# A Mamba layer on one core: eight units' products with B made by ScalarE and TensorE from u turned, instead of five by matmuls with diagonals

## What is computed

```
xi = silu(conv(in_proj(x)));  dt, Bm, Cm = split(x_proj(xi));  dt = softplus(dt_proj(dt) + dt_b)
dA  = exp(dt[..., None] * A)                      # (b, t, 512, 16)
dBx = (dt * xi)[..., None] * Bm[:, :, None, :]    # u = dt * xi
h_t = dA_t * h_(t-1) + dBx_t;   y_t = sum over the 16 states of h_t * C_t
y   = (y + xi * D) * silu(z);   out_proj, sigmoid
```

## Time and profile before

| | us |
|---|---|
| median of 3 runs (lowest, highest) | 4762.65 (4761.55, 4768.12) |
| span of the profiled execution, first to last instruction | 4760.7 |
| both passes of the Mamba layer, from 82 on | 3338 |
| a chunk of the backward pass, one of the forward pass | 105.5, 103.2 |
| join and feed-forward net | 1341 |

### The profile page before, as it was taken

One profiled execution on the slowest core, in us unless ns is written; L12 is line 12 of the kernel. 1 busy time (PEld: TensorE's weight loads), 2 busy tenths in 40 slices (PEclk: granted clock), 3 DMA queues, 4 the chain that ended last, 5 costly groups with the idle time before them and its releaser, 6 DMA issues. The chain is left out here.

```text
span 4760.7 us, 67108 instructions
## 1 busy us (share of the span) xinstructions
PE 4479.5 (94%) x24932; PEld 3395.1 (71%) x24932; DVE 3894.2 (82%) x4126; ACT 3109.7 (65%) x5158; POOL 3320.9 (70%) x1559
## 2 busy tenths in 40 slices
PE   7999999999999989999999999998799999999999
PEld 3666666666666666667666667666688888888888
DVE  5999999999999999999999999999854444444452
ACT  6777777777777777777777777777444444444443
POOL 4999999999999999999999999999820000000000
PEclk9999999999999999999999999999999999999999
DMA  7544444444444444444444444444231111010100
GB/s 271 178 142 141 134 151 132 136 134 134 143 139 134 155 132 138 129 139 139 131 147 140 129 130 136 143 142 156 103 123 32 36 32 36 32 36 32 36 23 10
DMA packets 297736, 545.76 MB, mean 115 GB/s; under 512 B 101888, under 2 KB 186624, under 8 KB 262784
## 3 DMA queue, kind: packets, MB, share of 16 engines
q1 hardware_dynamic: 296512, 529.91, 35.6%
q10 hardware_dynamic: 896, 11.54, 0.7%
HBM read 502.77 MB, written 50.14 MB: 116 GB/s over the span
## 5 line engine op out<-in xcount | busy, mean ns | idle before, releaser
L1400 DVE TENSOR_TENSOR_SCAN m_h<-bank,m_state,m_dBx 128x512 f32<-128x512 f32 x1512 | 1841.2, 1265 | 35.0 <-ACT bank L1145 27.2
L868 PEld LDWEIGHTS bank<-ident,m_h 128*128 128x128 f32 x8192 | 980.9, 143 | 417.2 <-issue 345.8
L868 PE MATMUL bank<-ident,m_h 128*128 128x128 f32 x8192 | 1197.6, 276 | 12.9 <-DVE m_h L1408 12.8
L1283 POOL TENSOR_TENSOR m_dBx<-u,m_Bs 128x1024 f32<-128x1024 f32 x432 | 1016.4, 2377 | 0.4 <-DMA m_Bs<-b_dram 0.2
L1283 POOL TENSOR_TENSOR m_dBx<-m_u,m_Bs 128x1024 f32<-128x1024 f32 x432 | 1015.5, 2371 | 1.2 <-DMA m_Bs<-b_dram 1.0
L1294 POOL TENSOR_TENSOR m_h<-m_h,m_Cs 128x1024 f32<-128x1024 f32 x384 | 909.4, 2368 | 105.8 <-ACT m_state L1077 105.1
L1408 DVE TENSOR_TENSOR m_h<-m_h,bank 128x1024 f32<-128x1024 f32 x640 | 767.0, 1198 | 51.7 <-PE bank L850 51.4
L1145 ACT ACTIVATE bank<-m_dt,cols 128x512 f32<-128x512 f32 x864 | 584.8, 688 | 225.2 <-DVE m_h L1400 223.7
L1145 ACT ACTIVATE bank<-dt,cols 128x512 f32<-128x512 f32 x864 | 584.1, 688 | 193.6 <-DVE m_h L1400 191.6
L302 POOL TENSOR_TENSOR mvj<-mvj,norm_c 128x4 f32<-128x4 f32 x16 | 16.5, 1032 | 969.0 <-DVE mvj L263 969.0
L731 PE MATMUL bank<-hT,w_in 128*128 128x512 f32 x1024 | 547.4, 630 | 113.1 <-ACT hT L998 105.8
(11 more groups left out here) (177 smaller groups left out, 5847.1 us busy)
## 6 DMA issues: line engine op xcount, KB each, us to landing
m_Bs<-b_dram SPq DMA_DIRECT2D x256, 1024.0 KB, 6.3
m_Cs<-c_dram SPq DMA_DIRECT2D x384, 256.0 KB, 3.7
m_dg<-d_dram SPq DMA_DIRECT2D x160, 256.0 KB, 3.9
xx<-in_x SPq DMA_DIRECT2D x16, 512.0 KB, 4.9
xn_dram<-xx SPq DMA_DIRECT2D x16, 512.0 KB, 4.5
yb_dram<-m_ysb SPq DMA_DIRECT2D x16, 512.0 KB, 5.0
xx<-xn_dram SPq DMA_DIRECT2D x16, 512.0 KB, 3.8
x_dram<-m_ysb SPq DMA_DIRECT2D x16, 512.0 KB, 5.0
```

Of the source, the lines that this page charges most:

```text
L868: mm = pe.matmul(YB[b][:, o:o + P], h[:, k % NH, m, tok:tok + P], ident[:, :], start=(s == 0 and o == 0), stop=False, is_transpose=True, s ...
L1283: pool.tensor_tensor(dBx[:, dbx_ring(ch, k) % NDBX, :, :], u[ch.batch][:, m, :], Bs[:, k // BP % 2, k % BP, :].unsqueeze(1).broadcast_to(( ...
L1400: dve.tensor_tensor_scan(o, decays, share, initial, ALU.mult, ALU.add).then_inc(S["scan"], 1)
```

## The change

- `A_UNITS` is now eight units, four in each half: 8, 11, 14 and 18, 21, 24, 27, 30. GpSimd makes 24 B products for a chunk (27 before).
- `P_UNITS` goes from 12 to 14 units. VectorE makes 18 C products (20 before), GpSimd 14.
- No diagonals: `store_diagonals`, `load_d`, the tensor `d_dram` and its first filling go. In their place ScalarE scales uT by B, which now lies along the partitions as a column of `Ct`: four ACTIVATEs of 128 x 256 for a unit (`scale_u`), at slots 2k - 5 to 2k - 2, into `uB`. TensorE turns uB back into the PSUM bank at slots 2k - 2 and 2k - 1 (`fill_a`).
- u of both halves is turned: two more turns by TensorE, two more copies by ScalarE.
- SyncE's list is in another order, without the loads and stores of diagonals.

```diff
-      J_Y: (45, 60, 14, 17), J_OUT: (31, 40), J_UT: (25, 26)}
+      J_Y: (45, 60, 14, 17), J_OUT: (31, 40), J_UT: (25, 26), J_UZ: (5, 7)}
+TURNS = ((J_UZ, AT_UZ), (J_UT, AT_UT))
-P_UNITS = (2, 3, 5, 9, 13, 15, 16, 19, 20, 22, 23, 27)
-A_FIRST, A_STEP, NA = 19, 3, 5
-A_UNITS = tuple(A_FIRST + A_STEP * i for i in range(NA))
+P_UNITS = (1, 4, 5, 7, 9, 11, 13, 16, 17, 20, 21, 23, 27, 29)
+A_UNITS = (8, 11, 14, 18, 21, 24, 27, 30)
+NA = len(A_UNITS)
+AT_US = (-5, -4, -3, -2)
...
                 load_c(ch, 4)
+                if norms(ch, 2):
+                    store_xn(ch.go(2))
                 load_b(ch, 4)
                 load_c(ch, 5)
-                load_b(ch, 5)
                 load_c(ch, 6)
-                if norms(ch, 2):
-                    store_xn(ch.go(2))
-                load_c(ch, 7)
-                load_b(ch, 6)
                 if has(ch, 1):
                     store_b(ch.go(1))
-                load_d(ch, 2)
+                load_b(ch, 5)
+                load_c(ch, 7)
                 load_c(ch, 8)
+                load_b(ch, 6)
...
                     if m == 0:
-                        if i == 0:
-                            wait_drained(pe, ch, J_UT[1])
-                        pe.wait_ge(d_in[n % NDG], 16 * (n // NDG) + 16)
+                        pe.wait_ge(S["u_scaled"], n + 1)
                     pe.wait_ge(S["scan"], tile - NDA + 1)
                     for s in range(TS):
-                        mm = pe.matmul(DA[tile % NDA][:, s * P:(s + 1) * P], uT[:, s, m * P:(m + 1) * P],
-                                       dg[:, n % NDG, s, :], start=True, stop=True)
+                        mm = pe.transpose(DA[tile % NDA][:, s * P:(s + 1) * P], uB[:, s, m * P:(m + 1) * P], ident[:, :])
...
+            def scale_u(ch, g):
+
+                for i, k in enumerate(A_UNITS):
+                    for t in range(TS):
+                        if g != 2 * k + AT_US[t]:
+                            continue
+                        n = ch.at(NA, i)
...
+                            wait(act, S["a_fill"], 2 * n)
+                        ins = act.activation(uB[:, t, :], uT[:, t, :], ACT.Copy,
+                                             scale=Ct[:, ch.batch, t, k % DS:k % DS + 1])
+                        if t == TS - 1:
+                            ins.then_inc(S["u_scaled"], 1)
...
                     if k == EVAC[0]:
                         evacuate(ch, 0)
+                    scale_u(ch, k)
                     if has(ch, -1):
                         tail(ch.go(-1), k)
```

More of the change, by code:

```diff
@@ L556, in store_b @@
                 sp.dma_start(c_dram[ch.batch], dbB[B0 + DS:B0 + 2 * DS, :]).then_inc(S["b_st"], 16)
-            def store_diagonals(ch):
-                wait_drained(sp, ch, J_B)
-                if ch.first():
-                    sp.sem_inc(S["go"], 1)
-                    sp.wait_ge(S["d_init"], 16 * BATCH * NA)
-                s = B0 + A_FIRST - DS
-                by_diagonal = d_dram[ch.batch].rearrange("i (p w) -> i p w", w=DIAG)
-                for n in range(TS):
-                    sp.dma_start(by_diagonal[:, :, n * P], dbB[s:s + A_STEP * (NA - 1) + 1:A_STEP, n * P:(n + 1) * P],
-                                 allow_slow_non_contiguous=True).then_inc(S["d_st"], 16)
             def load_b(ch, j):
@@ L796, in turn_u @@
             def turn_u(ch, g, m):
-                if g == AT_UT[m]:
-                    if m == 0:
-                        pe.wait_ge(S["u_ready"], ch.at(2, 2))
-                    turn(J_UT[m], lambda s: u[ch.batch][:, 2 + m, s * P:(s + 1) * P], ch)
+                for half, (jobs, at) in enumerate(TURNS):
+                    if g == at[m]:
+                        if m == 0:
+                            pe.wait_ge(S["u_ready"], ch.at(2, half + 1))
+                        turn(jobs[m], lambda s: u[ch.batch][:, 2 * half + m, s * P:(s + 1) * P], ch)
             def fill_a(ch, g):
@@ L1029, in front @@
                     wait(act, S["b_st"], ch.at(32, 0))
-                    if not ch.first():
-                        act.sem_inc(S["go"], 1)
-                        act.wait_ge(S["d_st"], ch.at(64, 0))
                     rows = B0 + 2 * DS
@@ L1137, in decay @@
                     if m == 0:
[L1138 removed]
+                        wait(act, S["turned"], ch.at(NU, j - NH + 1))
                     out = h[:, j % NH, m, :]
@@ L1148, in keep_uT @@
             def keep_uT(ch, k):
[L1149 to L1153 removed]
+                for half, (jobs, at) in enumerate(TURNS):
+                    for m in range(2):
+                        if k != at[m] + ACT_LAG:
+                            continue
+                        wait_filled(act, ch, jobs[m])
+                        if m == 0:
+                            act.sem_inc(S["go"], 1)
+                            wait(act, S["u_scaled"], ch.at(NA, sum(k < half * DS for k in A_UNITS)))
+                        b = BANK[jobs[m]]
                         act.copy(uT[:, :, m * P:(m + 1) * P], FB[b][:, :].rearrange("p (t n) -> p t n", n=P)
                                  ).then_inc(drain[b], 1)
+            def scale_u(ch, g):
+                for i, k in enumerate(A_UNITS):
+                    for t in range(TS):
+                        if g != 2 * k + AT_US[t]:
+                            continue
+                        n = ch.at(NA, i)
+                        if t == 0:
+                            if i == 0:
+                                wait_drained(act, ch, J_C)
+                                act.sem_inc(S["go"], 1)
+                            if i == 0 or A_UNITS[i - 1] // DS < k // DS:
+                                for j in TURNS[k // DS][0]:
+                                    wait_drained(act, ch, j)
+                                    act.sem_inc(S["go"], 1)
+                            wait(act, S["a_fill"], 2 * n)
[3 more added lines that the diff above has]
+                            ins.then_inc(S["u_scaled"], 1)
             def rows(g):
```

54 lines of the change are left out of this document (16 added, 38 removed).

## The result

| | us |
|---|---|
| before, median of 4 runs beside it | 4762.98 (4761.55 to 4768.12) |
| after, median of 4 runs | 5156.15 (5153.4 to 5162.0) |
| ratio, 95% interval | 1.0824 (1.0809 to 1.0839) |
| span of the profiled execution after | 5152.0 |
| forecast | 4860 (4768 to 4915) |

A forecast was written before the change was run, and what follows sets the result against it. VectorE was taken as the bound, waiting for ScalarE and TensorE. 31 x (0.9 + 2.7) + 0.9 - 15 x 0.9 = 99 us on the profiled 4760.7 gave 4860, range 4768 to 4915.

The forecast's parts named there:

- What goes: VectorE sheds two C products, 2.2 us a chunk, net in slots 23 and 31; this was to turn into waiting.
- two and two: Slots 4 to 20: C products of units 1 and 4 leave VectorE, 2 and 3 come; no cost.
- three out, three in: Slots 32 to 67: C products of units 17, 21, 29 leave VectorE, 15, 19, 22 come; its work unchanged.
- What comes on ScalarE: Scalings at 0.40 us start to start plus two copies of uT: 13.8 us more ScalarE work a chunk.
- TensorE waiting for ScalarE: Rival: TensorE waits for the scaling at slot 2k - 2, 1 to 2 us more a chunk, 4890 to 4920; chance 0.12.
- Slots 21 to 32: Five scalings in ScalarE's unbroken chain of decays delay scan 32: +0.9 us a chunk, between 0.3 and 1.4.
- The load of B: Slots 32 to 67: load for units 20 to 23, behind stores, makes GpSimd and scan 68 late: +2.7 us a chunk.
- VectorE's own work in between is unchanged: Between scans 32 and 68: VectorE's work stays the same, so GpSimd's lateness adds 2.7 us to the former 55.93.
- The rest of the edits: TensorE gains 24 turns, 3.8 us a chunk, hidden in its idle time; diagonals' transfers, unit 8 and copies cost nothing.
- -0.9 in slot 5: Backward chunks: the stall at slot 68 takes in a wait for spread C in slot 5, -0.9 in 15 chunks.
- The range's own ends: Ends of the chain and load terms, 31 x (0.3 + 1.4) = 53 to 31 x (1.4 + 4.0) = 167: 4813 to 4925.

The follow-up runs named there:

- e7: e2 with the twelve C units of the kernel before, so VectorE keeps its 20 C products: 4857.59 us.
- e2: The changed kernel with no scalings, u turned as it is and B left out of the eight units' products: 4914.99 us.
- the other two pairs: The changed kernel against itself with the C units of before (5156.15, 5102.90 us), and e1 against e1 with those units (5050.35, 4966.24 us).
- e1: The changed kernel with a second buffer for the scaled u, the last chunk keeping one: 5050.35 us.
- e3: The kernel before with 32 idle scalings added to a chunk, output unread and no waits of their own: 4925.56 us.
- e10: e3 with only the 16 idle scalings of the first half (slots 11 to 34): 4855.55 us.
- e4: The changed kernel with the load of B for units 20 to 23 again ahead of the stores of the next chunk's B and C: 5158.15 us.
- e6: e2 without the turns of u's first half and their copies by ScalarE: 4912.56 us.
- e9: e7 with only the turned units 18, 21, 24, 27, 30, without the turns of u's first half, 27 B products on GpSimd: 4815.57 us.
- e15: The kernel before with its five turned units moved one unit down, to 18, 21, 24, 27, 30, diagonals kept: 4865.51 us.

## Why the prediction was wrong

The direction was right, and so was its first reading: VectorE sets the pace, waits for decays, and ScalarE's 25 us of idle are not where they are needed. The size was not. Where the time went, as the mean over forward chunks (backward ones give +2.3, +5.3 and +5.3):

| stretch | before | after | forecast |
|---|---|---|---|
| scan 4 to the end of scan 21 | 28.8 | 30.9 | +0 |
| end of scan 21 to scan 32 | 18.6 | 23.5 | +0.9 |
| scan 32 to scan 68 | 55.9 | 61.6 | +2.7 |

By its own steps:

- **What goes** (2.2 us of VectorE a chunk, not gained): right that the products of slots 23 and 31 give nothing, and right that "two and two" in slots 4 to 20 is nearly even (e7 against e2: 1.1 each, four times, and 0.3 over in a forward chunk). The first failed step is "three out, three in", taken as even in slots 32 to 67 because it counts products and not what stands behind them. Of the three that go, one covered the wait of scan 52 and one gave 0.2 to 0.3; the three that come cost 1.13 each. e7 against e2 measures the set: 52 us where the forecast has 0 (53 and 74 in the other two pairs).
- **What comes on ScalarE**: right. Forecast 0.49 long and 0.40 from start to start; the row of the scaling (busy us, mean ns of one, idle before) has 500 ns, and its neighbours start 0.40 to 0.42 later:

```profile
L1145 ACT ACTIVATE m_uB<-m_uT,m_Ct 128x256 f32<-128x256 f32 x1024 | 511.7, 500 | 237.1 <-PE bank L786 237.1
```

- The Trainium skill, "ScalarE: Activation LUTs", section "What ACT_TABLE_LOAD costs", gives it without bounds: 186 ns, 0.833 ns for a column and 93 for a pointer operand, an estimate of 492 ns. The trace's 500 agrees.
- **The same row holds the second failed step, the largest that had no term.** 237.1 us of idle ahead of the scaling, for TensorE's fill. The prediction named the wait for the fill nowhere. It listed TensorE waiting for ScalarE as a rival with a chance of 0.12 and 1 to 2 us a chunk, and not the other half of the handshake, ScalarE waiting for TensorE, with the decays behind it. e1 measures it: 111 us, 3.6 a chunk. The rival's own wait exists too, 74.6 us in 32 places, and e1 keeps it (74.7); what it costs no run separates.
- **Slots 21 to 32** (+0.9 a chunk, 28 us): mechanism right, term mis-sized. The stretch grew by 5.0, and the waits at scans 25 and 32 by 5.0 in the chunk shown. The scalings' share of the whole change, 130 us by e1 and e2 or 161 by e3, is 4.2 to 5.4 a chunk. Only the five scalings in this stretch were priced, and three ahead of the copy to dbB; the others were taken to fall into idle time. They don't: e10 shows nearly half the cost in the second half's scalings, and the changed kernel waits 1.8, 0.8 and 1.1 for the decays of scans 52, 53 and 57 of a forward chunk, before none.
- **The load of B** (+2.7 a chunk, 84 us): the mechanism came as forecast to a few tenths up to GpSimd's product, and e4 finds its price to be 0. The step that failed is the one from there to scan 68, "VectorE's own work in between is unchanged": VectorE had waits of its own in that stretch, which made it 5.7 us longer, and two latenesses side by side count once. At scans 44 and 68, where the forecast saw VectorE waiting for GpSimd, it does not wait. The Trainium skill's fit in "SBUF — State Buffer", section "The DMA setup-cost knee", weighed in the prediction, gave an estimate of 4.4 for the load; from issue to GpSimd's start took 4.8, nearer to that than to my 5.9, which would have moved only this term.
- **The rest of the edits**: the two turns and copies of u are hidden, right (e6: no difference). But TensorE did not gain 24 matmuls a chunk, it lost 16. The fills by diagonals have two in the trace for each of the kernel's 40 multiplications in a chunk, those by turning one for each of 64:

```profile
L815 PE MATMUL bank<-m_dg,m_uT 128*128 128x128 f32 x2560 | 346.3, 279 | 22.0 <-DVE m_h L1400 18.6
```

```profile
L786 PE MATMUL bank<-ident,m_uB 128*128 128x128 f32 x2048 | 321.4, 281 | 106.4 <-ACT m_uB L1145 74.6 <-DVE m_h L1392 31.7
```

- "-0.9 in slot 5" had the wrong sign: VectorE's wait there is 3.22 in the backward chunk shown, 0.92 before, in the mean over a pass 2.5 to 2.7 against 0.7 to 1.6, and its waits for spread C went from 51.4 to 147.6. This wait also differs from chunk to chunk before (0 to 2.9), so the chunks of a pass are not alike to a few tenths: from the third to the last but one they last 103.7 to 106.7 backward and 102.3 to 104.9 forward.
- **A turned unit** had no price beyond TensorE's 0.16 a turn, a third failed step: three more of them cost 46 us, and moving the five by one unit 53 to 103.
- The range's own ends leave out the slot 5 term that the sum has, and the upper one adds up to 4928, not 4925; neither matters here.
- That e9's 53 us are places is read from waits which e15 has too; no run takes the diagonals out and leaves the units where they were.

The range failed because its ends bounded two terms, and three of the five that mattered had no term.

## What to carry to other kernels

Where the engines of a kernel run lists in order and each is within some per cent of full, price a move by its slot: an operation that stands before a wait is free to keep and gives nothing when it goes, and its place elsewhere costs in full. For each new pair of producer and consumer write down both waits, the consumer's for the data and the producer's for the buffer, and what stands behind each on its engine. Idle time of an engine that others follow is not room: put idle instructions of the planned size there and measure (here 12.8 us of them cost 5.4) before building the change, and do the same with only the work moved, since here the aim itself (one C product off VectorE) cost 26 us.
